# A quarter of an output product moved ahead of the projection in TensorE's loop over heads

## What is computed

```
h = x * rsqrt(mean(x*x) + eps) * norm_w
Q, K, V = h @ wq.T, h @ wk.T, h @ wv.T      (each plus a low-rank term)
Q, K = rope(Q), rope(K)                     16 heads of 128
scores = Q K^T / sqrt(128), a row sees itself and the 63 before it
attn = softmax(scores);  out = attn V
out = out @ wo.T                            (plus a low-rank term)
```

## Time and profile before

| what | value |
|---|---|
| median of three runs | 1182.82 us (1181.33 to 1185.87) |
| the profiled execution | 1184.07 us |
| its span, first to last instruction | 1182.2 us |
| PE busy | 1010.5 us, 85% |
| DVE busy | 849.3 us, 72% |
| ACT busy | 673.5 us, 57% |
| POOL busy | 604.3 us, 51% |
| the attention stage on TensorE | from about 285 to about 895 us of the span |

### The profile page before, as it was taken

The page is one execution under the profiler, slowest core; times in us unless marked ns, Lnnn a source line. Parts: engine busy times, 40 slices in busy tenths (PEclk is TensorE's granted clock), DMA queues, the critical chain, the costliest instruction groups (busy, mean ns, idle before and its releaser), DMA issues.

```text
span 1182.2 us, 21240 instructions
## 1 busy us (share of the span) xinstructions
PE 1010.5 (85%) x6229; PEld 677.7 (57%) x6229; DVE 849.3 (72%) x2233; ACT 673.5 (57%) x1720; POOL 604.3 (51%) x596
## 2 busy tenths in 40 slices
PE   4966798845788899899999999999978889999984
PEld 2544543323456576567666766666664568886442
DVE  4586566845587768867668888888874787776677
ACT  1532344514657765876966556656664777775332
POOL 0468465512666567554544555554542145552774
PEclk9988999977999999999999999999998999999997
DMA  9777599977454257041110011210016745554443
GB/s 342 297 202 283 96 330 301 298 257 224 76 131 99 94 113 159 13 96 38 50 59 4 34 36 37 85 37 1 1 61 212 202 119 146 145 142 101 134 123 101
DMA packets 96956, 156.00 MB, mean 132 GB/s; under 512 B 12208, under 2 KB 67248, under 8 KB 94032
## 3 DMA queue, kind: packets, MB, share of 16 engines
q1 hardware_dynamic: 77120, 115.48, 29.8%
q0 software_dynamic: 19728, 39.21, 14.9%
HBM read 104.91 MB, written 45.02 MB: 127 GB/s over the span
## 4 chain that ended last, share of the span: by engine, by line
PE 38%; DVE 18%; ACT 17%; issue 10%; DMA 5%; DVEq 4%; POOL 3%; ACTq 2%; POOLq 1%; SPq 1%
PE ps L1234 5%; ACT arena L1482 5%; PE ps L1068 4%; ACT arena L1459 3%; PE ps L1180 3%; DMA arena<-in_wdn 3%; PE ps L883 3%; PE ps L1128 2%; PE ps L1197 2%; DVE arena L2001 2%; ACT arena L1458 2%; PE ps L1081 2%; ACT arena L1475 2%; PE ps L1252 2%; PE ps L1097 2%
## 5 line engine op out<-in xcount | busy, mean ns | idle before, releaser
L2287 POOL TENSOR_TENSOR arena<-arena 128x512 f32<-128x512 f32 x128 | 160.4, 1270 | 144.3 <-ACT arena L1459 143.5
L1068 PE MATMUL ps<-arena 128*128 128x512 f16 x768 | 178.5, 382 | 19.5 <-ACT arena L1459 19.5
L2294 POOL TENSOR_TENSOR arena<-arena 64x512 f32<-64x512 f32 x128 | 137.1, 1071 | 113.2 <-DVE arena L1946 109.5
L1458 ACT ACTIVATE arena<-ps 64x512 f32<-64x512 f32 x128 | 76.0, 594 | 154.3 <-DVE arena L1918 150.2
L1068 PEld LDWEIGHTS ps<-arena 128*128 128x128 f16 x768 | 73.0, 98 | 119.3 <-ACT arena L1459 32.7
L2332 POOL DMA_INDIRECT wvo<-xn_d,idx x79 | 75.9, 960 | 113.6 <-PE ps L1224 96.9
L1482 ACT ACTIVATE arena<-arena 128x192 f32<-128x192 f32 x256 | 112.5, 444 | 2.4 <-DVEq L1941 2.4
L1081 PE MATMUL ps<-wvo,arena 128*128 128x512 f16 x384 | 94.6, 383 | 12.2 <-issue 5.9
L1097 PE MATMUL ps<-arena 128*128 128x192 f32 x512 | 96.7, 332 | 7.2 <-DVE arena L1924 5.4
L1128 PE MATMUL ps<-wvo,arena 128*128 128x256 f16 x768 | 96.4, 278 | 1.8 <-DVE arena L1958 1.4
L1924 DVE TENSOR_TENSOR arena<-arena 128x512 f32<-128x512 f32 x128 | 88.2, 729 | 7.9 <-POOL arena L2287 7.9
(11 more groups left out here) (293 smaller groups left out, 2166.1 us busy)
## 6 DMA issues: line engine op xcount, KB each, us to landing
arena<-wqk_d SPq DMA_DIRECT2D x16, 1024.0 KB, 5.2
arena<-in_wgu SPq DMA_DIRECT2D x32, 384.0 KB, 11.0
y_d<-wvo SPq DMA_DIRECT2D x79, 128.0 KB, 2.4
z_d<-wvo SPq DMA_DIRECT2D x8, 1024.0 KB, 4.2
z_d<-wvo SPq DMA_DIRECT2D x2, 4096.0 KB, 27.8
arena<-in_wdn SPq DMA_DIRECT2D x32, 192.0 KB, 14.2
arena<-z_d SPq DMA_DIRECT2D x12, 512.0 KB, 4.4
arena<-z_d POOLq DMA_DIRECT2D x12, 512.0 KB, 7.3
```

Source lines behind the costliest of these rows:

```text
L1068: last = pe.matmul(ps[s][:, :], wqk[gg][:, s * DC + c, w, hh * DH:(hh + 1) * DH], hx[bb][:, :, x, c * P:(c + 1) * P], start=(c == 0 and w ...
L1458: nc.scalar.activation(qk_s[0:64, s], ps[s][64:P, :], ACT.Copy)
L2287: nc.gpsimd.tensor_tensor(qk_s[:, s], qk_s[:, s], sin, ALU.mult).then_inc(sin_done, 1)
L2294: nc.gpsimd.tensor_tensor(pm[u][rows, at:at + SEQ].rearrange("p (t n) -> p t n", t=TPB), pp[u][rows, :, at:at + P], ri[rows].unsqueeze(2). ...
```

## The change

In the loop over heads on TensorE the call of `output_quarter` moves from behind the projection, the transposes and the counting matmuls to the head's beginning. Nothing else moves, and no instruction is added or removed.

```diff
             for h in range(NH):
+                for n, q in quarters_at(h):
+                    output_quarter(n, q)
                 if h + 2 < NH:
                     project(h + 2)
                 for t in tiles_at(FOLLOW_AT, h - 1):
...
                     pe.matmul(ps[2][:, NT * E1:2 * NT * E1], ones_bf[:, :], flat(mkA), start=True, stop=True).then_inc(counted, 1)
-                for n, q in quarters_at(h):
-                    output_quarter(n, q)
                 if h + 1 < NH:
                     scores(h + 1, (h + 1) % 2)
```

## The result

The changed kernel takes 1196.98 us as the median of 7 executions (1192.60 to 1202.96), the kernel before 1185.0 us in 7 (the three of the table before and four more). The ratio is 1.0103 with a 95% interval of 1.0068 to 1.0137: 12 us slower, 8 to 16 by the interval. The profiled execution took 1197.68 us, 13.6 more than the one shown before. The forecast of 1191 us (8.1 us more) had the direction, and two thirds of the size (12.2 us by the ratio). The 1196.98 us lie just under the upper end of its range, 1197; 2.2 of the 6 us between 1191 and 1196.98 are the median of the kernel before, which had been 1182.82 in the first three executions.

What follows compares the result with a forecast made beforehand. The prediction took the loop through VectorE and ScalarE as the bound, with slack on TensorE. Late scores of 3.0 us plus 5.1 us of lowered clock gave + 8.1 us, about 1191 us, range 1184.5 to 1197.

Steps and rivals of the forecast that it cites:

- TensorE has slack, the loop runs through VectorE and ScalarE: Main loop over heads: TensorE, 85% busy, is ahead of need in most heads; VectorE and ScalarE set the pace.
- The rival by which they are on the path: TensorE's 19.5 us of waits at the projection would cost time and go away: faster, 1163 us, chance 0.05.
- The quarter begins at L1958 + 0.78 and takes the head's slack: Quarters q = 0 in 15 heads start 0.78 us after L1958 starts; head 53 keeps 0.03 us of slack.
- Four direct losses of 0.6, 0.5, 0.3 and 1.6, 3.0 us in all: Heads 21, 29, 37 and 61: scores come too late for the engines waiting, 3.0 us together.
- Heads 13, 25 and 33 see their L1958 done within 0.1 us of the head's start: In these heads the moved quarter would hardly wait for VectorE's output_low, so no loss was counted.
- Five falls of the clock, 5.1 us: Pauses of 3 us or more before quarters in heads 5, 9, 17, 45, 61 halve TensorE's clock, costing 5.1 us.
- Which pauses fall: Pauses of 3 us or more before quarters were taken to halve TensorE's clock, those of 2.3 to 2.4 not.
- The four pauses of 2.3 to 2.4 us: Pauses before the quarters of heads 37, 49, 53 and 57: 6.5 us more if they halve the clock, counted as none.
- The price of a fall: Each 3.4 us of matmuls at half clock takes 1.7 us more, less the head's slack.
- three quarters: Share of the 6.8 us clock loss taken, 5.1 us, as some half-clock stretches would begin inside the pause.
- The sign in the clock row: The profile's granted-clock row would show slices under 9 around heads 5, 9, 17, 45 and 61.
- 1186 us: Time if TensorE's clock stays up and only the 3.0 us of late scores are lost, chance 0.25.

Runs made afterwards that it cites:

- q0_behind: Against the changed kernel, only quarters q = 1 to 3 stand at the head's beginning, q = 0 stays behind the projection: 1188.03 us, ratio 1.0003 to the kernel before.
- the filled kernel: The changed kernel with unread matmuls filling TensorE's pauses, placed ahead of the previous head's value product: ratio 1.0048 to the kernel before.
- changed_again: The changed kernel, unaltered, run and traced again on another chip beside the kernel before: ratio 1.0086, stage 621.2 us.
- the last batch: Final runs sharing one chip, where the kernel before took 1218.01 us; the changed kernel's ratio there was 1.0086.

## Why the prediction was right in kind and too small

- **TensorE has slack, the loop runs through VectorE and ScalarE.** Right. The 19.5 us at the projection went almost wholly (1.7 left) in the change itself, mostly (4.3 left) in `q0_behind`, and bought nothing. The rival by which they are on the path is out.
- **The quarter begins at L1958 + 0.78 and takes the head's slack.** Right, head 53 to a tenth of a microsecond. The quarters q = 2, which the forecast did not walk, wait too (2.12 us in head 43), and by `q0_behind` cost nothing.
- **Four direct losses of 0.6, 0.5, 0.3 and 1.6, 3.0 us in all.** Right: 0.5, 0.5, 0.3 and 1.6 to 1.7 in the filled kernel, where no fall of the clock mixes in.
- **"Heads 13, 25 and 33 see their L1958 done within 0.1 us of the head's start", so they cost nothing.** This step failed for head 13, a term put at nothing. The quarter indeed hardly waits there, but the projection that it now holds up releases a load of 1 MB, and that lands among GpSimd's row copies: 1.2 to 1.3 us. The walk over the heads followed TensorE and VectorE, and left out what SyncE's queue waits for.
- **Five falls of the clock, 5.1 us.** This is the term that was mis-sized. That pauses ahead of the quarters bring the clock down, and that this costs time, was right: the falls go when the pauses are filled. They cost 5.6 us in `changed_again` (0.5, 1.3, 1.7, 0.7 and 1.5 for the heads 5, 9, 37, 45 and 61; the terms are rounded) and 6.5 on the first profile of the changed kernel (1.2 in the heads 5 to 8, 1.3 in head 9, 0.7 in head 21 beyond its direct loss, 1.7 in head 37 beyond it, 0.7 in head 45, 0.9 in head 57). With the direct 3.0, head 13's 1.3 and 0.5 at the stage's start the latter makes the 11.4 but for rounding.
- **Which pauses fall: "The four pauses of 2.3 to 2.4 us [...] I take none of them", and all five of 3 us or more.** This choice failed in both directions. Head 37's pause (2.15 us) was followed by half clock in both traces of the changed kernel, head 57's (2.04) in one of them. Head 17's (3.52 us in both) was followed by none in either. Head 61's pause fell in one (3.39 us) and not in the other (2.86 us). That the number of falls came out near five is luck. The row that spoke against the choice was there: the forecast read the clock as full up to the stage's end, but the trace before has 6.8 us at half clock from 885.8 us. Behind a pause of 2.09 us that ends at 884.19, 1.43 us of matmuls and a second pause, of 1.41 us, were enough for a fall (the lines stand below).
- **The price of a fall: 1.7 us less the head's slack, times three quarters.** The 1.7 us are right where the forecast used them, at the scores: 1.68 us later in the heads 5, 9, 37 and 45. The three quarters were to allow for stretches that begin inside the pause; in `changed_again` they began within 0.9 us after the quarter's start in those four heads, so nearly all of each lay on matmuls. What the forecast lacks is slack further on in VectorE's pass. The passes get 0.5, 1.3 and 0.7 us in the heads 5, 9 and 45, where 1.2, 1.7 and 1.5 were forecast ahead of the three quarters. In head 45 VectorE's wait for L1475 at its next L1958 shrinks from 1.40 us (filled) to 0.69. Head 37 pays its 1.7 us in full. So two errors offset each other: falls in the forecast heads cost less than assumed, and head 37's, which was taken at nothing, made up for it.
- **What would show it.** The quarter in head 53 waited 2.31 us, L1068's wait fell to 1.7 us, the period of the table heads stayed at 8.95 us where no fall stands. VectorE's waits at the scores in the heads 21 and 29 did not grow: the lateness moved to the `cosine` before them, though the heads lost the half microsecond as forecast. The sign in the clock row failed: of the slices around the heads 5, 9, 17, 45 and 61 only head 5's is under 9. 3.4 us at half clock leave 0.94 of a slice of 29.9 us, which prints as 9, so an unchanged row would not have spoken for 1186 us either.

The pause at the end of the stage in the trace before, and the stretch behind it:

```profile
884.19 1.43 PE L1116 MATMUL ps<-arena 128*128 128x192 f32 x8 [2.09 <-DVE arena L1952]
```

```profile
885.80:892.60 6.80, 5.56 (x27) 3.94 (x28) 0.91 (x2) 0.46 (x1) 0.00 (x0) 0.50 0.00 0
```

In one sum: forecast 3.0 + 5.1 = 8.1. Measured 3.0 of direct lateness, 1.3 for the load behind head 13, 5.6 and 6.5 for the clock in the two traces, and half a microsecond at the stage's start that other kernels show too: a stage 10.4 and 11.4 us longer. The term missed is head 13's, the term mis-sized the clock's, by 0.5 to 1.4 us. What the first profile lost outside the stage, 2.2 us, was not taken apart; in the two profiles of the last batch (1217.54 and 1226.71 us) the program outside the stage is 1.3 us shorter instead.

What stays open is why some pauses drop the clock and others do not. Neither their length alone nor the head explains it in these traces, as the last section counts.

## What to carry to other kernels

On an engine that works in order, put an instruction that waits behind the work that doesn't need its data, even where the engine seems to have slack: here the move took 17.8 us of waits out of one row and cost 12 us of time, since the slack was needed to cover the wait. Before moving a step, list every semaphore that it and the steps it delays count up, transfers included; the one missed here was a load on another queue. And look where the engine that sets the pace waits for a result, and put work that can come later behind that result: that gave 0.5% where only those heads were changed and 0.2% where all were, with overlapping intervals.

## What the runs showed of the hardware

In the 14 traces, from 40 to 580 us of the stage, TensorE has 47 pauses of 2.01 to 3.52 us between matmuls. Behind 26 of them, or already inside the pause, a stretch at 1.2 GHz began (3.4 us long, once 6.8), at most 1.7 us after the pause's end; 21 were followed by full clock. By length: 9 of 23 under 2.4 us, 9 of 12 from 2.4 to 3.0, 4 of 4 from 3.0 to 3.45, 4 of 8 from 3.45 on. No stretch at half clock stands there without such a pause. With the pauses ahead of the quarters q = 0 cut to 0.85 us and less, none stood between 40 and 600 us of the stage in one execution and one, behind a pause of 2.75 us that was not filled, in another. The Trainium skill ("TensorE: Matmul & The Clock Gate", section "What's actually happening") has idleness bring the lower level back; the traces agree that it can, and show besides that the same pause in the same head does it in one execution and not in another: head 57's, 2.04 us and 2.02 us in the two traces of the changed kernel, did in the first and not in the second, and head 17's, 3.47 to 3.52 us in four traces, never did.

A stretch of 3.4 us at half clock that lay on matmuls made the scores behind it 1.68 us later. What it cost the kernel was between nothing (the three falls of `q0_behind`) and 1.7 us (head 37), by the slack of the engines that wait for TensorE.
